# Decoder layer on one core: products with 64-row heads as two row tiles of TensorE, state sums as two column tiles, without zero-padded copies

## The chip, the cores and the metric

The kernel runs on one core of a Trainium2 chip. The metric is the time of one execution on the device in microseconds (us), lower is better; of several runs the median counts.

## The reference

One decoder layer over x of shape (8, 512, 256) in fp32: a gated slot attention with 4 heads of 64 and 64 slots, a cross attention with 16 heads of 16 over 64 keys for each batch, and a feed-forward part with 8 experts of which each token takes 2. Only the first two parts are touched. Cut to what matters:

```python
def step(carry, inp):                       # one token of the slot attention, for each of 4 heads
    hk, hv = carry
    q_t, k_t, v_t, s_t, g_t = inp
    ge = exp(g_t)
    hk = hk * ge[:, :, None, :] + k_t[..., :, None] * s_t[..., None, :]
    logits = einsum('bhk,bhkm->bhm', q_t * scale, hk)
    p = softmax(logits)
    hv = hv * ge[..., :, None] + s_t[..., :, None] * v_t[..., None, :]
    o_t = einsum('bhm,bhmv->bhv', p, hv)
...
scores = einsum('bhqd,bhkd->bhqk', Q, K) * scale + bias      # cross attention, 16 heads of 16
```

The kernel does the recurrence in chunks of 128 tokens. Inside a chunk the part `q k^T` of a head (causal, 128 tokens by 128) stands for the sum over earlier tokens, and likewise `p s^T` for the read of the values; what came before the chunk is held in the states hk and hv, two heads side by side as diagonal blocks of 64 by 64.

## The kernel before

The 4096 tokens are 32 chunks of 128 (`NCH`), four to a batch. The first stage loops over the chunks; the second, after it, runs the experts over 40 groups of 256 rows and isn't touched. Every engine has its own program, an order written out by hand: its `step(run)` lists the pieces of work of one chunk, and `run(lag, work)` does the piece for the chunk that lies `lag` behind. So one step of the loop does the slot attention of chunk n (lag 0 and 1), the cross attention of chunk n-1 and n-2, and the routing of n-3 and n-4. Steps are unrolled for the first 8 chunks; then a loop runs 6 times over 4 steps, and 4 last steps follow. Semaphores order the engines among each other; an engine never starts a piece before the one above it in its list.

In one step the slot attention of a chunk is a chain through all engines. VectorE (DVE) normalises the chunk (`f_xn`), TensorE (PE) turns and projects it, ScalarE (ACT) and DVE make the gates (`g_s`, `down`, `s_s`), PE turns k and s (`ks_columns`), ACT copies them out (`k_z`, `s_z`), PE makes the products `scores`, DVE masks them (`a_s`, line 902), PE makes `logits`, DVE and ACT the softmax (`lg`, `b_e`, `b_p`), PE turns `b_p` (`p_columns`), ACT copies it (`p_t`), PE makes the products `mix`, DVE masks them (`bt_s`, line 936), and PE makes `sum_states` and `read_out`. After `bt_s` DVE begins the next step with the statistics of the next chunk.

Heads have 64 rows, and a product over them is made with all 128 rows of the array: `k_z` and `s_z` hold one head each in a tile of 128 rows of which the other 64 are zeros, written once. The cross attention does the same with `k_bd`, in which GpSimd (POOL) lays the keys of 8 heads of 16 rows side by side, with zeros elsewhere; it is made once for each batch (`keys`, line 490). `sum_states` makes blocks of 128 by 128 of which only the diagonal blocks of 64 are used.

PSUM has eight banks, and `turns` says which results use a bank in which order; `bank_left` makes PE wait until the one before it has been read.

Of the kernel before, what the change touches and what calls it, by code (L numbers as in the profile page):

```python
# [29 lines left out]
ALU = mybir.AluOpType  # L30
ACT = mybir.ActivationFunctionType
AX = mybir.AxisListType
F32 = mybir.dt.float32
# [5 lines left out]
P = 128  # L39
# [33 lines left out]
def decoder_layer(nc, x, qpos, kpos, mask, ctx_t, wq, wk, wv, wf, gnorm, wo,  # L73
# [3 lines left out]
    with ctx:  # L77
# [18 lines left out]
        def part1(name, shape, dt=F32):  # L96
            return tiles1.enter_context(nc.sbuf_tensor(name, shape, dt))
# [7 lines left out]
        diag16 = part1("diag16", [P, HPT])  # L105
        pair_of = part1("pair_of", [P, 2])
# [34 lines left out]
        k_z, s_z = part1("k_z", [P, H, P]), part1("s_z", [P, H, P])  # L141
# [18 lines left out]
        k_bd = part1("k_bd", [P, KT, HPT, KL])  # L160
# [37 lines left out]
        bank = [ctx.enter_context(nc.psum_tensor(f"bank{i}", [P, 512], F32)) for i in range(8)]  # L198
# [11 lines left out]
        tile = {t: bank[i][:, :] for i, turn in enumerate(turns) for t, _ in turn}  # L210

# [7 lines left out]
        def sems(names):  # L219
            return [sem(t) for t in names.split()]  # L220
# [22 lines left out]
        down_ok, decay_ok, kz_ok = sems("down_ok decay_ok kz_ok")  # L243

        left = dict(f_cols=f_cols_ok, qk=qk_ok, vf=g_ok, gates=gates_ok, decay_cols=h_ok, ks_cols=ks_ok, sums=z_ok,
                    scores=a_ok, logits=lg_ok, p_cols=p_ok, mix=mix_ok, read=bo_ok, o_cols=o_ok, y=x1_ok,
# [68 lines left out]
        CONSTS = 15 + XH  # L315
# [105 lines left out]
        def _(pool):  # L421
# [34 lines left out]

            pool.wait_ge(consts_step, CONSTS)

# [118 lines left out]
        def _(act):  # L577
# [9 lines left out]
            def two(t):  # L587
                return t.rearrange("p (k t) -> p k t", k=2)
# [19 lines left out]
            def ks_columns(n, c, b):  # L608

                if later(n, 1):  # L610
                    act.wait_ge(mix_mm, n)
                else:
                    act.wait_ge(halves_zeroed, 6)
# [157 lines left out]
        def _(dve):  # L771
            for t in (k_z, s_z, *hk, *hv):
                dve.memset(t[:, :, :], 0.0).then_inc(halves_zeroed, 1)
# [55 lines left out]
            causal_h = causal[:, :].rearrange("p (a t) -> p a t", a=1).to_broadcast([P, H, P])  # L829
# [68 lines left out]
            def causal_scores(n, c, b):  # L898
                if later(n, 1):
                    dve.wait_ge(logits_mm, n)  # L900
                dve.wait_ge(scores_mm, n + 1)
                dve.tensor_tensor(a_s[:, :, :], tile["scores"].rearrange("p (h t) -> p h t", h=H), causal_h, ALU.mult)\
                   .then_inc(a_ok, 1)
# [91 lines left out]
            def x_scores(n, c, b):  # L995
                dve.wait_ge(bias_ok, n + 1)
                dve.wait_ge(xs_mm, n + 1)
                if later(n, 1):
                    dve.wait_ge(ex_ok, n)
                for k in range(2):  # L1000
                    last = dve.tensor_tensor(sc[:, 8 * k:8 * k + 8, :],
                                             tile[f"x_scores{k}"].rearrange("p (h k) -> p h k", h=HPT),
                                             bias[:, 8 * k:8 * k + 8, :], ALU.add)
                last.then_inc(sc_ok, 1)
# [220 lines left out]
        def _(pe):  # L1225
# [72 lines left out]
            def sum_states(n, c, b):  # L1298

                pe.wait_ge(v_ok, n + 1)  # L1300
                bank_left(pe, "sums", n)
                for m in range(2):
                    cols = slice(m * P, (m + 1) * P)
                    product(tile["sums"][:, cols], [(k_s[:, c % 2, cols], s_s[:, c % 2, cols])])
                    last = product(tile["sums"][:, D + m * P:D + (m + 1) * P], [(s_s[:, c % 2, cols], v_s[:, c % 2, cols])])
                last.then_inc(sums_mm, 1)

            def scores(n, c, b):
                pe.wait_ge(kz_ok, n + 1)
                bank_left(pe, "scores", n)  # L1310
                for h in range(H):
                    last = product(tile["scores"][:, h * P:(h + 1) * P], [(k_z[:, h, :], q_t[:, c % 2, h // 2, :])])
                last.then_inc(scores_mm, 1)
# [25 lines left out]
            def mix(n, c, b):  # L1339
                pe.wait_ge(p_ok, n + 1)  # L1340
                bank_left(pe, "mix", n)
                for h in range(H):
                    last = product(tile["mix"][:, h * P:(h + 1) * P], [(s_z[:, h, :], p_t[:, h // 2, :])])
                last.then_inc(mix_mm, 1)
# [31 lines left out]
            def x_scores(n, c, b):  # L1376

                pe.wait_ge(xq_ok, n + 1)
                pe.wait_ge(kbd_ok, b * KT + KT)
                for k in range(KT):  # L1380
# [154 lines left out]
```

## Time and profile before

| | |
|---|---|
| median of 3 runs | 1630.9 us (1628.46 to 1631.94) |
| span of the profiled execution, first to last instruction | 1613.6 us |
| busy in the span: PE, DVE, ACT, POOL | 88%, 65%, 41%, 28% |
| mean granted TensorE clock | 0.942 |

The span is 17.3 us below the median; that part lies before the first and behind the last instruction. The profiled execution has no total time of its own in the records besides its span. A chunk's step takes some 25 to 27 us, so the first stage is about 890 us of the span and the experts the rest. An fp32 product shows as two matmul records on PE (and two weight loads on PEld), so counts of PE rows are double the number of products. PE rows of the timeline give the start of a group of records, the time from its first start to its last end, and how many there are; the next row can start before that end, since matmuls overlap.

### The profile page before, as it was taken

What the parts mean: (1) busy time and instruction counts of PE and PEld (TensorE: products, weight loads), DVE (VectorE), ACT (ScalarE), POOL (GpSimd) and SP (SyncE); (2) the same over time, 40 slices, a digit from 0 to 9 for tenths busy, and PEclk for the clock granted to TensorE, in tenths of its full rate; (3) what the DMA queues carried; (4) which work ended last, traced back from release to release, by engine and by line L of the source; (5) the groups of instructions that cost most, each with busy time, mean ns of one, the idle gap of its engine ahead of it and who ended that gap; (6) DMA issues with size and microseconds to landing.
All of it is one profiled execution on the core that took longest, in us unless ns stands there. A gap on an engine that the chain in (4) does not pass through costs nothing. (4 is left out here: it accounts for less than half of the span.)

```text
span 1613.6 us, 31497 instructions
## 1 busy us (share of the span) xinstructions
PE 1425.9 (88%) x10360; PEld 1281.7 (79%) x10360; DVE 1049.4 (65%) x3246; ACT 656.3 (41%) x1626; POOL 446.7 (28%) x510
## 2 busy tenths in 40 slices
PE   6798988888888888888886499999999999999995
PEld 4576767767676667676775499999999999999995
DVE  3568787777788787878886465555555465555442
ACT  1345344444444343534342344444344344444331
POOL 1224233333333342423332211222121121222212
PEclk8899999998999999989997699999999999999998
DMA  9100000000000000000000513223141323241211
GB/s 311 53 9 29 15 29 15 29 15 28 15 28 19 24 27 15 28 14 29 14 21 12 195 27 86 58 54 93 29 116 29 107 38 108 38 109 28 40 21 20
DMA packets 65998, 79.65 MB, mean 49 GB/s; under 512 B 9793, under 2 KB 59330, under 8 KB 65856
## 3 DMA queue, kind: packets, MB, share of 16 engines
q1 hardware_dynamic: 51264, 59.05, 11.8%
q0 software_dynamic: 14592, 18.91, 7.0%
q8 instruction: 64, 1.05, 0.3%
q14 instruction: 78, 0.64, 0.1%
HBM read 44.15 MB, written 33.83 MB: 48 GB/s over the span
## 5 line engine op out<-in xcount | busy, mean ns | idle before, releaser
L755 ACT ACTIVATE h_a<-bank 128x256 f32<-128x256 f32 x320 | 122.5, 383 | 357.6 <-PE bank L1235 355.5
L1167 DVE TENSOR_TENSOR h_f<-bank,h_a 128x256 f32<-128x256 f32 x320 | 135.5, 424 | 156.5 <-ACT h_a L755 152.0
L461 POOL TENSOR_TENSOR idle_g<-half 128x1 f32<-128x1 f32 x112 | 23.5, 209 | 608.5 <-DVE y_s L1186 411.9
L1235 PE MATMUL bank<-xe_t_hi,w_even_hi 128*128 128x256 f32 x640 | 180.4, 282 | 0.0
L1235 PE MATMUL bank<-xe_t_hi,w_odd_hi 128*128 128x256 f32 x640 | 178.6, 279 | 0.0
L1235 PE MATMUL bank<-xe_t_lo,w_even_hi 128*128 128x256 f32 x640 | 178.5, 279 | 0.0
L1235 PE MATMUL bank<-xe_t_hi,w_even_lo 128*128 128x256 f32 x640 | 178.5, 279 | 0.0
L1235 PE MATMUL bank<-xe_t_lo,w_odd_hi 128*128 128x256 f32 x640 | 177.0, 276 | 0.0
L1235 PE MATMUL bank<-xe_t_hi,w_odd_lo 128*128 128x256 f32 x640 | 176.9, 276 | 0.0
L742 ACT ACTIVATE h_t_hi<-h_f 128x256 fp32r<-128x256 f32 x320 | 131.8, 412 | 28.8 <-DVE h_f L1167 28.7
L1174 DVE TENSOR_TENSOR h_t_lo<-h_f,h_t_hi 128x256 fp32r<-128x256 f32 x320 | 133.5, 417 | 6.1 <-ACT h_t_hi L742 5.0
L565 POOL DMA_INDIRECT out_dram<-y_s,token x80 | 125.2, 1565 | 27.3 <-issue 20.2
L1235 PEld LDWEIGHTS bank<-xe_t_lo,w_even_hi 128*128 128x128 f32 x640 | 122.0, 191 | 0.0
L1235 PEld LDWEIGHTS bank<-xe_t_hi,w_even_hi 128*128 128x128 f32 x640 | 121.9, 190 | 0.0
L1235 PEld LDWEIGHTS bank<-xe_t_hi,w_even_lo 128*128 128x128 f32 x640 | 121.8, 190 | 0.0
L1235 PEld LDWEIGHTS bank<-xe_t_hi,w_odd_hi 128*128 128x128 f32 x640 | 120.3, 188 | 0.0
L1235 PEld LDWEIGHTS bank<-xe_t_lo,w_odd_hi 128*128 128x128 f32 x640 | 120.3, 188 | 0.0
L1235 PEld LDWEIGHTS bank<-xe_t_hi,w_odd_lo 128*128 128x128 f32 x640 | 120.2, 188 | 0.0
L1235 PE MATMUL bank<-w_in,f_xnt 128*128 128x512 f32 (+1 forms) x256 | 99.7, 513 | 1.9 <-ACT f_xnt L585 1.9
L468 POOL TENSOR_TENSOR f_rstd<-f_var,neg_half 128x1 f32<-128x1 f32 x32 | 17.6, 551 | 291.2 <-DVE f_var L814 291.2
L1184 DVE CAST token<-about 128x1 uint32<-128x1 f32 x80 | 8.6, 149 | 130.8 <-PE bank L1235 130.8
L1235 PE MATMUL bank<-w_odd_hi,h_t_lo 128*128 128x256 f32 x320 | 88.5, 277 | 0.0
(220 smaller groups left out, 3961.8 us busy)
## 6 DMA issues: line engine op xcount, KB each, us to landing
raw<-in_w SPq DMA_DIRECT2D x24, 1024.0 KB, 8.5
expert_rows<-empty SPq DMA_DIRECT2D x4, 2580.0 KB, 21.5
xe<-expert_rows SPq DMA_DIRECT2D x40, 258.0 KB, 2.7
xin<-in_x SPq DMA_DIRECT2D x32, 128.0 KB, 2.3
out_dram<-x SPq DMA_DIRECT2D x32, 128.0 KB, 1.9
out_dram<-y_s,token POOLq DMA_INDIRECT x80, 3.8
mask_i<-in_mask SPq DMA_DIRECT2D x32, 32.0 KB, 1.7
expert_rows<-r_xn,send POOLq DMA_INDIRECT x64, 2.8
```

The costliest lines, as they stand in the source:

```text
L461: return pool.tensor_tensor(idle_g[:, i:i + 1], half[:, 0:1], half[:, 0:1], ALU.add)
L468: pool.tensor_tensor(rstd[:, :], var[:, :], neg_half[:, 0:var.shape[1]], ALU.pow).then_inc(done, 1)
L565: pool.indirect_dma_start(out=out, out_offset=bass.IndirectOffsetOnAxis(ap=token[par][a][:, :], axis=0), in_=y_s[:, par, a, :], in_offset= ...
L742: act.activation(h_t[0][:, par, f, :], h_f[:, f % 2, :], ACT.Copy).then_inc(h_hi_ok, 1)
L755: act.activation(h_a[:, f % 2, :], bank[2 + f % 4][:, 0:GS], ACT.Silu).then_inc(silu_ok, 1)
L1167: dve.tensor_tensor(h_f[:, f % 2, :], bank[2 + f % 4][:, GS:2 * GS], h_a[:, f % 2, :], ALU.mult)\
L1174: dve.tensor_tensor(h_t[1][:, par, f, :], h_f[:, f % 2, :], h_t[0][:, par, f, :], ALU.subtract)\
L1184: dve.tensor_copy(token[par][a][:, :], about[:, par, a, 0:1])
L1235: last = pe.matmul(dst, lhs, rhs, start=(i == 0), stop=(i == len(pairs) - 1))
```

## The change

The zero-padded copies go. `k_t` and `s_t` hold two heads on top of each other, rows 0 to 63 and 64 to 127, in one copy each. A product takes rows 0 to 63 or 64 to 127 of both operands, so that it uses one half of the array's rows (a row tile); two products next to each other in the program use different halves and write to different banks (`scores0`/`scores1`, `mix0`/`mix1`, `x_scores0`/`x_scores1`). `k_bd` has half as many columns, as 4 heads share a row half. The sums take 64 columns of weights and write 64 partitions, heads 0 and 2 to the lower, 1 and 3 to the upper half (a column tile). The blocks off the diagonal aren't written any more; the bank is zeroed once at the start. The turns of the banks change with the new names. DVE reads two banks in one operation (`two_banks`).

```diff
+        diag4 = part1("diag4", [P, HPT // 2])
-        k_z, s_z = part1("k_z", [P, H, P]), part1("s_z", [P, H, P])
+        k_t, s_t = part1("k_t", [P, PAIRS1, P]), part1("s_t", [P, PAIRS1, P])
-        k_bd = part1("k_bd", [P, KT, HPT, KL])
+        k_bd = part1("k_bd", [P, KT, HPT // 2, KL])
...
-            [("xo_cols", 3), ("qk", 0), ("scores", 0)],
+            [("xo_cols", 3), ("qk", 0), ("scores0", 0), ("mix0", 0)],
+            [("f_cols", 0), ("decay_cols", 0), ("scores1", 0), ("mix1", 0)],
             [("vf", 0), ("ks_cols", 0), ("logits", 0), ("r_cols", 3)],
             [("o_cols", 1), ("values", 2), ("sums", 0)],
-            [("f_cols", 0), ("decay_cols", 0), ("mix", 0)],
-            [("x_scores1", 2), ("p_cols", 0)],
-            [("x_scores0", 2), ("gates", 0), ("y", 1), ("e_cols1", 2), ("xq", 1)],
+            [("x_scores0", 2), ("p_cols", 0)],
+            [("x_scores1", 2), ("gates", 0), ("y", 1), ("e_cols1", 2), ("xq", 1)],
...
-                            .to_broadcast([P, HPT, KL]),
-                            diag16[:, :].rearrange("p (h a) -> p h a", a=1).to_broadcast([P, HPT, KL]),
+                            .to_broadcast([P, HPT // 2, KL]),
+                            diag4[:, :].rearrange("p (h a) -> p h a", a=1).to_broadcast([P, HPT // 2, KL]),
...
-                for t, dst, done in ((0, k_z, kz_ok), (1, s_z, ks_ok)):
-                    for i in range(2):
-                        rows = slice(M * i, M * i + M)
-                        last = act.activation(dst[rows, i::2, :], two(tile["ks_cols"][rows, t * D:(t + 1) * D]), ACT.Copy)
-                    last.then_inc(done, 1)
+                act.activation(k_t[:, :, :], two(tile["ks_cols"][:, 0:D]), ACT.Copy).then_inc(kt_ok, 1)
+                act.activation(s_t[:, :, :], two(tile["ks_cols"][:, D:2 * D]), ACT.Copy).then_inc(ks_ok, 1)
...
-                dve.tensor_tensor(bt_s[:, :, :], tile["mix"].rearrange("p (h t) -> p h t", h=H), causal_h, ALU.mult)\
+                dve.tensor_tensor(bt_s[:, :, :].rearrange("p (m i) t -> p i m t", i=2), two_banks, causal_h, ALU.mult)\
...
-                for m in range(2):
-                    cols = slice(m * P, (m + 1) * P)
-                    product(tile["sums"][:, cols], [(k_s[:, c % 2, cols], s_s[:, c % 2, cols])])
-                    last = product(tile["sums"][:, D + m * P:D + (m + 1) * P], [(s_s[:, c % 2, cols], v_s[:, c % 2, cols])])
+                for a, (keys, rows) in enumerate(((k_s, s_s), (s_s, v_s))):
+                    for h in range(H):
+                        i, cols = h % 2, slice(h * M, (h + 1) * M)
+                        last = product(tile["sums"][M * i:M * i + M, a * D + h * M:a * D + (h + 1) * M],
+                                       [(keys[:, c % 2, cols], rows[:, c % 2, cols])])
...
+            def by_pair(names, keys, queries):
+                for m in range(PAIRS1):
+                    for i in range(2):
+                        rows = slice(M * i, M * i + M)
+                        last = product(tile[names[i]][:, m * P:(m + 1) * P], [(keys[rows, m, :], queries[rows, m, :])])
+                return last
...
                 for k in range(KT):
-                    bank_left(pe, f"x_scores{k}", n)
-                    last = product(tile[f"x_scores{k}"], [(xq_t[:, k, :], k_bd[:, k, :, :].rearrange("p h k -> p (h k)"))])
+                    for i in range(2):
+                        rows = slice(P // 2 * i, P // 2 * (i + 1))
+                        last = product(tile[f"x_scores{i}"][:, k * D:(k + 1) * D],
+                                       [(xq_t[rows, k, :], k_bd[rows, k, :, :].rearrange("p h k -> p (h k)"))])
```

On PE, in a step with all lags, from the query projection of the cross attention (`x_xnt,xw`) to the turning of the next chunk (`ident,f_xn`), the program before reads so (out<-in, columns written; semaphores that a row waits for in brackets):

```order
L1235 MATMUL bank<-x_xnt,xw 128x128 x3
L1235 MATMUL bank<-p_t,s_z 128x128 [waits h_ok,mix_ok,f_cols_ok,p_ok]
L1235 MATMUL bank<-p_t,s_z 128x128 x3
L1235 MATMUL bank<-s_s,k_s 128x128 [waits xo_ok,z_ok,o_ok,v_ok]
L1235 MATMUL bank<-v_s,s_s 128x128
L1235 MATMUL bank<-s_s,k_s 128x128
L1235 MATMUL bank<-v_s,s_s 128x128
L1319 MATMUL bank<-hv,p_t 128x128 [waits bo_ok,et_ok,p_ok]
...
L1235 MATMUL bank<-k_bd,xq_t 128x512 [waits x1_ok,gates_ok,et_ok,sc_ok,xq_ok,kbd_ok]
L1235 MATMUL bank<-k_bd,xq_t 128x512 [waits p_ok,sc_ok]
L1229 MATMUL bank<-ident,f_xn 128x128 [waits h_ok,mix_ok,f_cols_ok,f_normed]
```

and with the change:

```order
L1239 MATMUL banks<-x_xnt,xw 128x128 x3
L1239 MATMUL banks<-p_t,s_t 128x128 [waits f_cols_ok,mix_ok,h_ok,a_ok,qk_ok,xot_ok,p_ok]
L1239 MATMUL banks<-p_t,s_t 128x128 x3
L1239 MATMUL banks<-s_s,k_s 64x64 [waits xo_ok,z_ok,o_ok,v_ok]
L1239 MATMUL banks<-s_s,k_s 64x64 x3
L1239 MATMUL banks<-v_s,s_s 64x64 x4
L1331 MATMUL banks<-hv,p_t 128x128 [waits bo_ok,et_ok,p_ok]
...
L1239 MATMUL banks<-k_bd,xq_t 128x256 [waits gates_ok,sc_ok,x1_ok,p_ok,et_ok,xq_ok,kbd_ok]
L1239 MATMUL banks<-k_bd,xq_t 128x256 x3
L1233 MATMUL banks<-ident,f_xn 128x128 [waits a_ok,h_ok,mix_ok,f_cols_ok,f_normed]
```

No piece changes its place: four `mix` products stay four, four sums of 128 by 128 become eight of 64 by 64, and two score products of 512 columns become four of 256.

On ACT, the copies of the turned k and s stood before between `ex` (the exponent of the cross attention) and `e_t`:

```order
L696 ACTIVATE ex<-sc 128x1024 [waits et_mm,scd_ok]
L618 ACTIVATE k_z<-bank 64x2x128 [waits ks_mm,mix_mm]
L618 ACTIVATE k_z<-bank 64x2x128
L618 ACTIVATE s_z<-bank 64x2x128 x2
L626 ACTIVATE e_t<-bank 128x512 [waits et_mm,av_mm]
```

and now:

```order
L696 ACTIVATE ex<-sc 128x1024 [waits et_mm,scd_ok]
L618 ACTIVATE k_t<-banks 128x256 [waits ks_mm,mix_mm]
L619 ACTIVATE s_t<-banks 128x256
L626 ACTIVATE e_t<-banks 128x512 [waits et_mm,av_mm]
```

Four copies over 64 rows have become two over 128 rows, in the same place.

## Rows read from the trace of the kernel before

**Rows 1.** Windows, both stages: window, us; busy (count) by engine; PEclk; DMA share, GB/s
```profile
60.00:860.00 800.00, 682.80 (x4188) 558.31 (x4188) 632.40 (x2134) 345.67 (x850) 278.81 (x289) 0.94 0.07 21
1000.00:1600.00 600.00, 594.83 (x5216) 594.43 (x5214) 318.68 (x810) 245.95 (x630) 127.30 (x144) 1.00 0.28 63
```

**Rows 2.** Line 936 (`bt_s`) on DVE over the whole span, and its idle time
```profile
L936 DVE TENSOR_TENSOR bt_s<-bank,causal x32: 690/692/692, 44.7 to 852.0; 128x512 f32<-128x512 f32 x32
...
  PE bank L1235: 62.9, 32
```

**Rows 3.** Timeline of DVE: start, duration, work, idle before and its releaser
```profile
404.42 0.69 DVE L936 TENSOR_TENSOR bt_s<-bank,causal 128x512 f32<-128x512 f32 x1 [2.87 <-PE bank L1235]
...
425.97 0.43 DVE L923 TENSOR_TENSOR b_p<-b_e,up 128x256 f32<-128x256 f32 x1 [0.55 <-ACT b_e L683]
428.79 0.69 DVE L936 TENSOR_TENSOR bt_s<-bank,causal 128x512 f32<-128x512 f32 x1 [1.04 <-PE bank L1235]
```

**Rows 4.** Timeline of PE from the query projection to the next chunk
```profile
401.28 1.91 PE L1235 MATMUL bank<-x_xnt,xw 128*128 128x128 f32 x8
402.99 1.32 PE L1235 MATMUL bank<-p_t,s_z 128*128 128x128 f32 x8
404.15 0.39 PE L1235 MATMUL bank<-s_s,k_s 128*128 128x128 f32 x2
...
406.33 1.94 PE L1235 MATMUL bank<-k_bd,xq_t 128*128 128x512 f32 x4
408.10 0.38 PE L1229 MATMUL bank<-ident,f_xn 128*128 128x128 f32 x2
```

**Rows 5.** Timeline of PE, the same place one step later
```profile
426.73 1.06 PE L1235 MATMUL bank<-x_xnt,xw 128*128 128x128 f32 x8
427.62 1.06 PE L1235 MATMUL bank<-p_t,s_z 128*128 128x128 f32 x8
```

**Rows 6.** Windows at these two places, columns as in rows 1
```profile
401.00:402.00 1.00, 1.00 (x7) 1.00 (x6) 0.51 (x2) 0.77 (x2) 0.00 (x0) 0.50 0.00 0
...
427.00:428.00 1.00, 1.00 (x12) 1.00 (x11) 0.68 (x3) 0.49 (x2) 0.00 (x0) 1.00 0.00 0
```

**Rows 7.** Line 902 (`a_s`) on DVE over the whole span, and its idle time
```profile
L902 DVE TENSOR_TENSOR a_s<-bank,causal x32: 690/691/692, 35.9 to 843.8; 128x512 f32<-128x512 f32 x32
...
  PE bank L1235: 2.9, 3
```

**Rows 8.** Groups by line and shape, 400 to 503 us: busy, mean ns, idle before
```profile
L1235 PE MATMUL bank<-s_s,k_s 128*128 128x128 f32 x16 | 3.1, 275 | 0.0
...
L1235 PEld LDWEIGHTS bank<-s_s,k_s 128*128 128x128 f32 x16 | 2.4, 192 | 0.0
```

**Rows 9.** Timeline of PE where it waits or slows inside a step
```profile
414.12 0.18 PE L1235 MATMUL bank<-both,before 128*128 128x8 bf16 x1 [1.20 <-DVE both L1082]
...
414.55 0.70 PE L1235 MATMUL bank<-g_s,tri_half 128*128 128x256 f32 x2 [0.23 <-DVE g_s L849]
...
418.99 1.16 PE L1235 MATMUL bank<-q_t,k_z 128*128 128x128 f32 x8 [0.36 <-ACT k_z L618]
...
423.70 0.44 PE L1229 MATMUL bank<-ident,x_xn 128*128 128x128 f32 x2 [0.99 <-DVE x_xn L818]
...
441.44 1.22 PE L1235 MATMUL bank<-g_s,tri_half 128*128 128x256 f32 x2 [0.23 <-DVE g_s L849]
```

**Rows 10.** Lines 490 (`k_bd`) and 513 (`bias`) on POOL, 983 (`hid`) on DVE
```profile
L490 POOL TENSOR_TENSOR k_bd<-k_all,diag x16: 1045/1066/1082, 53.4 to 788.7; 128x512 f32<-128x512 f32 x16
...
L513 POOL TENSOR_TENSOR bias<-dist,slopes x32: 1900/1902/2028, 64.0 to 867.5; 128x1024 f32<-128x1024 f32 x32
...
L983 DVE TENSOR_SCALAR hid<-mask_i x32: 182/184/1105, 62.1 to 865.9; 128x64 f32<-128x64 int32 x32
```

**Rows 11.** Timeline of POOL and DVE where both meet
```profile
470.30 2.08 POOL L490 TENSOR_TENSOR k_bd<-k_all,diag 128x512 f32<-128x512 f32 x2
...
471.35 1.09 DVE L983 TENSOR_SCALAR hid<-mask_i 128x64 f32<-128x64 int32 x1
```

More of the change, by code:

```diff
@@ L196, in decoder_layer @@
         y_s = sb("y_s", [P, 2, 2, D])
[L198 removed]
+        banks = ctx.enter_context(nc.psum_tensor("banks", [P, 8 * 512], F32))
+        bank = [banks[:, i * 512:(i + 1) * 512] for i in range(8)]
         turns = [
             [("counts", 4), ("e_cols0", 2), ("read", 0)],
[L202 removed]
+            [("xo_cols", 3), ("qk", 0), ("scores0", 0), ("mix0", 0)],
+            [("f_cols", 0), ("decay_cols", 0), ("scores1", 0), ("mix1", 0)],
             [("vf", 0), ("ks_cols", 0), ("logits", 0), ("r_cols", 3)],
             [("o_cols", 1), ("values", 2), ("sums", 0)],
[L205 to L207 removed]
+            [("x_scores0", 2), ("p_cols", 0)],
+            [("x_scores1", 2), ("gates", 0), ("y", 1), ("e_cols1", 2), ("xq", 1)],
             [("r_logits", 4), ("xy", 3), ("x_cols", 1)],
@@ L242, in decoder_layer @@
             "topi_ok both_ok gap_ok re_ok cnt_mm place_ok taken_ok slots_ok route_step halves_zeroed")
-        down_ok, decay_ok, kz_ok = sems("down_ok decay_ok kz_ok")
+        down_ok, decay_ok, kt_ok = sems("down_ok decay_ok kt_ok")
         left = dict(f_cols=f_cols_ok, qk=qk_ok, vf=g_ok, gates=gates_ok, decay_cols=h_ok, ks_cols=ks_ok, sums=z_ok,
-                    scores=a_ok, logits=lg_ok, p_cols=p_ok, mix=mix_ok, read=bo_ok, o_cols=o_ok, y=x1_ok,
+                    scores0=a_ok, scores1=a_ok, logits=lg_ok, p_cols=p_ok, mix0=mix_ok, mix1=mix_ok, read=bo_ok, o_cols=o_ok, y=x1_ok,
                     x_cols=x_cols_ok, xq=xq_ok, x_scores0=sc_ok, x_scores1=sc_ok, e_cols0=et_ok, e_cols1=et_ok,
@@ L771, in _ @@
         def _(dve):
-            for t in (k_z, s_z, *hk, *hv):
+            dve.memset(tile["sums"], 0.0)
+            for t in (*hk, *hv):
                 dve.memset(t[:, :, :], 0.0).then_inc(halves_zeroed, 1)
@@ L901, in causal_scores @@
                 dve.wait_ge(scores_mm, n + 1)
-                dve.tensor_tensor(a_s[:, :, :], tile["scores"].rearrange("p (h t) -> p h t", h=H), causal_h, ALU.mult)\
+                dve.tensor_tensor(a_s[:, :, :].rearrange("p (m i) t -> p i m t", i=2), two_banks, causal_h, ALU.mult)\
                    .then_inc(a_ok, 1)
@@ L999, in x_scores, with quarter @@
                     dve.wait_ge(ex_ok, n)
[L1000 to L1003, printed above, removed]
+                for i in range(2):
+                    def quarter(t):
+                        return t[:, :, :].rearrange("p (k i j) l -> p i k (j l)", k=KT, i=2)[:, i, :, :]
+                    last = dve.tensor_tensor(quarter(sc), tile[f"x_scores{i}"].rearrange("p (k n) -> p k n", k=KT),
+                                             quarter(bias), ALU.add)
                 last.then_inc(sc_ok, 1)
@@ L1301, in sum_states @@
                 bank_left(pe, "sums", n)
-                for m in range(2):
-                    cols = slice(m * P, (m + 1) * P)
-                    product(tile["sums"][:, cols], [(k_s[:, c % 2, cols], s_s[:, c % 2, cols])])
-                    last = product(tile["sums"][:, D + m * P:D + (m + 1) * P], [(s_s[:, c % 2, cols], v_s[:, c % 2, cols])])
-                last.then_inc(sums_mm, 1)
-            def scores(n, c, b):
[L1309 to L1313, printed above, removed]
+                for a, (keys, rows) in enumerate(((k_s, s_s), (s_s, v_s))):
[3 more added lines that the diff above has]
+                                       [(keys[:, c % 2, cols], rows[:, c % 2, cols])])
+                last.then_inc(sums_mm, 1)
+            def by_pair(names, keys, queries):
[4 more added lines that the diff above has]
+                return last
+            def scores(n, c, b):
+                pe.wait_ge(kt_ok, n + 1)
+                for name in ("scores0", "scores1"):
+                    bank_left(pe, name, n)
+                by_pair(("scores0", "scores1"), k_t, q_t[:, c % 2, :, :]).then_inc(scores_mm, 1)
             def with_states(dst, queries, states, weights, rows, weights_ok, n):
@@ L1340, in mix @@
                 pe.wait_ge(p_ok, n + 1)
[L1341 to L1344, printed above, removed]
+                for name in ("mix0", "mix1"):
+                    bank_left(pe, name, n)
+                by_pair(("mix0", "mix1"), s_t, p_t).then_inc(mix_mm, 1)
             def read_out(n, c, b):
@@ L1379, in x_scores @@
                 pe.wait_ge(kbd_ok, b * KT + KT)
+                for i in range(2):
+                    bank_left(pe, f"x_scores{i}", n)
                 for k in range(KT):
-                    bank_left(pe, f"x_scores{k}", n)
-                    last = product(tile[f"x_scores{k}"], [(xq_t[:, k, :], k_bd[:, k, :, :].rearrange("p h k -> p (h k)"))])
+                    for i in range(2):
+                        rows = slice(P // 2 * i, P // 2 * (i + 1))
+                        last = product(tile[f"x_scores{i}"][:, k * D:(k + 1) * D],
+                                       [(xq_t[rows, k, :], k_bd[rows, k, :, :].rearrange("p h k -> p (h k)"))])
                 last.then_inc(xs_mm, 1)
```

9 lines of the change are left out of this document (5 added, 4 removed).

## Prediction

> **What bounds the kernel now.** I read the windows first. From 60 to 860 us, the chunk stage, PE is busy 682.8 of 800 us (85%) and DVE 632.4 (79%); in the expert stage PE is busy 594.8 of 600 [rows 1]. The expert stage is PE's and isn't touched, so everything below is about the chunk stage. No engine is full there, so I looked for the loop that closes from step to step. It is in the order of DVE's work: `bt_s` is DVE's last piece of a step, the next chunk's statistics come behind it, and the chain of that next chunk leads back to its own `bt_s`. From `bt_s` at 404.42 to the start of `b_p` at 425.97 are 21.55 us, in which DVE works nearly without a pause; then 2.82 us pass until the next `bt_s` at 428.79, and here DVE waits for PE, 1.04 us in this step and 2.87 in the one before [rows 3]. Over all 32 chunks this wait is 62.9 us [rows 2]. So a step is a DVE part of about 22 us and a tail in which DVE waits: turn `b_p`, copy it, make the query projection that stands ahead of `mix` on PE, make `mix`.
>
> Why is that tail short once and long once? In the step at 427 us the eight records of the query projection take 0.89 us to the start of `mix`, 0.111 us each [rows 5]; at 401 us they take 1.71 us, 0.214 each [rows 4]. The granted clock is 1.00 in the one and 0.50 in the other, that is 2.4 and 1.2 GHz [rows 6]. Ahead of this place PE has sat idle 0.99 us for `x_xn`, earlier 1.20 us for `both` [rows 9]. If all 32 tails were like the short one, the waits would come to 32 x 1.04 = 33.3 us instead of 62.9; 29.6 us are the price of the low clock in the tail.
>
> What isn't on this loop: the `scores` products. DVE waited for them three times in 32, 2.9 us in all [rows 7].
>
> **The change part by part.** The sum is made against the span of 1613.6 us; the median of the runs, 1630.9, lies 17.3 us above it, and I keep those 17.3.
>
> *Keys on POOL.* `k_bd` takes 1.066 us for 512 columns, `bias` 1.902 for 1024 [rows 10]: 0.836 us for 512 more columns, so 256 columns should take 1.066 - 0.418 = 0.65 us, and the two `k_bd` of a batch 1.30 instead of 2.08. While they run, from 470.30 to 472.38, DVE's `hid` begins at 471.35 and takes 1.09 us [rows 11] where 0.184 is the median and 1.105 the most [rows 10]; it ends when `k_bd` does. `hid` is in the DVE part of the loop. With `k_bd` done 0.78 us earlier it ends 0.78 earlier. Once for each of the seven batches after the first: **-5.5 us**. Bounds: 0, if something else stops `hid`, and 7 x 0.91 = -6.4.
>
> *Copies on ACT.* Two copies of 128 rows for four of 64 rows free `scores` from its wait of 0.36 us [rows 9]. `scores` isn't on the loop [rows 7], so **0**. A new wait is in its list: `scores1` uses the bank of `decay_cols`, so PE now also waits for `start_states` on DVE. That work stands well ahead of `a_s` on DVE, so it can't delay `a_s`; what is queued behind `scores` on PE, the `e_columns` of the cross attention, would be late by tenths of a us and has slack. 0.
>
> *`mix` as row tiles.* This is the one product in the tail. It has eight records of 128 columns before and eight after, 0.89 us at the high clock [rows 5]. No row shows two products at once in different halves of the array. Bounds: if the second record of one product runs beside the first of the next, eight records take five places, 0.55 us, a gain of 0.34; if nothing overlaps, 0. Against it stands the change of the array's shape between `x_xnt,xw` and `mix`. A matmul record lasts 275 ns though the next starts 111 ns later, and its weight load 192 ns, normally hidden [rows 8]. If a change of shape makes PE let the last product run out, 275 - 111 = 0.16 us come into the open; if the load can't start before that either, 0.16 + 0.19 = 0.36 us. So a tail moves between -0.34 and +0.36 us. Taking half of each, -0.17 + 0.16, gives **0** for 32 steps, with -11 and +12 us as ends.
>
> The Trainium skill speaks on both sides here. "TensorEngine Tiling (Array Packing)", Key Properties, says that tiles run independently, and also that a change of the tiling mode, not merely of the tile, drains TensorE. It gives no price of the drain; no row here shows one. By the first sentence alone the step would gain the 0.34 us, by both together it comes near nothing.
>
> *The other products.* `x_scores`, four records of 512 columns, takes 1.77 us from 406.33 to 408.10 [rows 4]; with full overlap five places of half the length, 1.11 us. `sums`, eight records at 0.111 us, become sixteen short ones; between 0.45 us saved and nothing. `scores` like `mix`. A step enters or leaves a tiled shape seven times (into `x_scores` and out, into `scores` and out, into `mix`, on to `sums`, out): 7 x 0.16 = 1.1 to 7 x 0.36 = 2.5 us against 0.34 + 0.34 + 0.66 + 0.45 = 1.8 us saved at best. For PE's busy time that is about even. Its direct worth is 0: behind `mix` PE runs on to `both`, for which it waits 1.20 us anyway [rows 9]. That wait is also the cover if PE gets slower there.
>
> *DVE's operations* over two banks keep their count of elements and so, I take it, their 0.69 us [rows 2, 7]. The zeroing at the start is shorter by one operation, under cover of the loads. 0.
>
> Sum: 1613.6 - 5.5 = 1608.1 us span, and 1625.4 with the 17.3 around it.
>
> **The rivals.**
>
> *Overlap is full and the drain small.* The tail gains 0.34 x 32 = 11 us, with `k_bd` 16 us. At the low clock the saving in `mix` is double, and if the stretches of low clock fall on fewer tails, half of the 29.6 us can go as well: 1630.9 - 16 - 15 = 1600. For it: each product's halves are independent and write to different banks. Against it: the shapes change every few products.
>
> *PE gets faster, and the clock pays for it (the other side).* PE doesn't get more work, it waits longer. If `sums`, `x_scores` and `mix` are done 1.4 us earlier, the idle time ahead of `both` grows from 1.20 to 2.6 us, and with `scores` earlier that ahead of `x_xn` from 0.99 [rows 9] to 1.5 or more. In the step where PE had waited longer there, the gate product ran on for 1.22 us instead of 0.70 [rows 9]. A tail at the low clock costs 1.5 to 1.8 us more than one at the high clock [rows 3]. The waits tell that about 18 of 32 are low (29.6 / 1.65). If 10 more go low, +16.5; less 5.5, that gives 1642. It decides as soon as more than three tails are added (3.3 x 1.65 = 5.5). For it: a low clock follows idle PE in this trace, and this change makes PE idle where it doesn't bind. Against it: the drains may fill that idle time.
>
> *The changes of shape are dear.* With 0.36 us or more ahead of `mix` and little overlap the tail grows by 0.36 to 0.45 us: 32 x 0.4 = 13, less 5.5: 1638.
>
> *The tiles don't run beside each other and shape costs nothing.* Then PE does the same, and only `k_bd` counts, or even that is eaten by the stretches of low clock, which fall elsewhere when the step's length changes: 1625 to 1631.
>
> **How the numbers follow.** The forecast, the array part near nothing and `k_bd` 5.5 us, has a chance of 0.35, its own range 1615 to 1634, since the place of the low stretches shifts with any change of the step's length and three tails more or less are 5 us. Full overlap 0.17; the clock 0.30; dear changes 0.12; nothing but `k_bd` or not even that 0.06. The range of 1602 to 1650 leaves out the far end of the first rival and of the second. Faster by over 0.2% (3.3 us, about what a measurement of this kernel tells from no change): 0.24 + 0.17 + 0.02 + 0.03 = 0.46. Slower: 0.02 + 0.23 + 0.10 = 0.35. Within 0.2%: the remaining 0.19.
>
> **What the profile of the changed kernel would show.** `k_bd` near 0.65 us and `hid` near 0.2 to 0.3 in all steps: the first term. The start-to-start time of the `mix` records, 0.111 us at clock 1.00 now: about 0.06 means overlap; a gap of some tenths ahead of the first record of `mix`, `sums` and `hv,p_t` shows the changes of shape. DVE's wait ahead of `bt_s`, 62.9 us over 32: it gathers all of the tail; steps with a wait of 1.0 and of 2.5 or more tell the share of low clocks. `scores` without a wait for `k_t`, and no wait of DVE for `a_s`. I would be wrong in sign if the granted clock of the chunk stage falls clearly under 0.94 [rows 1], or if `bt_s` and `a_s` take longer than 0.69 us over two banks.

## The result and the profile after

The changed kernel takes 1649.89 us (median of 4, 1646.17 to 1655.04) against 1629.68 us of the kernel before (median of 4, 1626.49 to 1631.94). The ratio is 1.0096, with a 95% interval of 1.0059 to 1.0133 (the two medians divided give 1.0124, inside the interval): slower by 1%, where I had forecast faster by 0.34%. A run more than 1.5% above the fastest of the same kernel is left out of every ratio.

The profiled execution of the changed kernel has a span of 1644.4 us, 1.8 us under its own time of 1646.17, and a mean granted clock of 0.906 against 0.942. The chunk stage, columns as in [rows 1]:

```profile
60.00:860.00 800.00, 676.49 (x4438) 549.39 (x4436) 612.50 (x2069) 317.35 (x774) 265.06 (x281) 0.88 0.07 20
1000.00:1600.00 600.00, 595.18 (x5228) 594.99 (x5227) 323.40 (x816) 250.47 (x642) 124.94 (x141) 0.99 0.29 64
```

PE is busy for 676 of the 800 us (683 before), at a granted clock of 0.88 instead of 0.94. The wait of DVE ahead of `bt_s`, which gathers the tail [rows 2], grew:

```profile
L937 DVE TENSOR_TENSOR bt_s<-banks,causal x32: 690/692/693, 41.8 to 878.5; 128x512 f32<-128x512 f32 x32
...
  PE banks L1239: 76.1, 32
```

76.1 us instead of 62.9. Of the 32 waits that make it up, 29 are longer than 1.7 us, where 18 were; the others are 0.80 to 0.92 us, where they were 1.04 to 1.16. From the first `bt_s` to the last the changed kernel takes 29.4 us more (41.8 to 878.5, against 44.7 to 852.0), so this wait holds 13.2 us of it and not the whole. The next largest part is DVE's wait ahead of `s_s`, which stands behind PE's gate products (waits of DVE from 40 to 890 us: total, times, longest; before, then changed):

```profile
DVE s_s L868 <- issue: 7.4, 20, 0.5
...
DVE s_s L869 <- issue: 13.5, 16, 1.8
...
DVE s_s L869 <- ACT down L671: 2.9, 6, 1.6
```

That is 16.4 us instead of 7.4. Reading two banks at once costs nothing (0.692 us both). The keys and `hid`, over the whole span, answer to [rows 10]:

```profile
L495 POOL TENSOR_TENSOR k_bd<-k_all,diag x16: 612/640/650, 55.4 to 812.0; 128x256 f32<-128x256 f32 x16
...
L984 DVE TENSOR_SCALAR hid<-mask_i x32: 183/185/299, 65.3 to 892.0; 128x64 f32<-128x64 int32 x32
```

0.64 us for half the columns, and `hid` takes 0.30 us at most where it took 1.105: this term came as worked out. Now PE in one step of the changed kernel, which answers to [rows 4] and [rows 9] (64*128 and 128*64 are the rows and columns of the array that a product takes, where 128*128 is all of it):

```profile
400.70 0.18 PE L1239 MATMUL banks<-both,before 128*128 128x8 bf16 x1 [1.82 <-DVE both L1086]
...
405.44 0.71 PE L1239 MATMUL banks<-q_t,k_t 64*128 64x128 f32 x8 [0.23 <-DVE hv L887]
406.08 1.24 PE L1406 MATMUL banks<-ident,ex 128*128 128x128 f32 x8
...
408.16 0.66 PE L1336 MATMUL banks<-s_s,a_s 128*128 128x64 f32 x4 [0.61 <-DVE a_s L903]
...
410.48 0.54 PE L1233 MATMUL banks<-ident,x_xn 128*128 128x128 f32 x2 [0.99 <-DVE x_xn L819]
410.81 3.47 PE L1239 MATMUL banks<-v_bd,e_t 128*128 128x34 f32 x16
...
414.98 1.91 PE L1239 MATMUL banks<-x_xnt,xw 128*128 128x128 f32 x8
416.82 1.03 PE L1239 MATMUL banks<-p_t,s_t 64*128 64x128 f32 x8
417.78 0.45 PE L1239 MATMUL banks<-s_s,k_s 128*64 128x64 f32 x8
...
419.98 1.14 PE L1239 MATMUL banks<-k_bd,xq_t 64*128 64x256 f32 x8
421.04 0.44 PE L1233 MATMUL banks<-ident,f_xn 128*128 128x128 f32 x2
```

`x_scores` takes 1.06 us from 419.98 to 421.04, instead of 1.77, and `scores` 0.64 from 405.44 to 406.08, so tiles do run beside each other. PE then waits longer: 1.82 us for `both` instead of 1.20, 0.61 us for `a_s` and still 0.99 for `x_xn`. What follows is slow: the sixteen records of `v_bd` take 3.3 us to the next row and the projection 1.84. The windows there say why:

```profile
406.00:407.00 1.00, 1.00 (x11) 0.75 (x8) 0.96 (x4) 0.00 (x0) 0.56 (x1) 1.00 0.74 253
...
411.00:412.00 1.00, 1.00 (x8) 1.00 (x6) 0.93 (x3) 0.38 (x1) 0.00 (x0) 0.50 0.00 0
...
415.00:416.00 1.00, 1.00 (x6) 1.00 (x6) 0.24 (x1) 0.62 (x2) 0.00 (x0) 0.50 0.00 0
```

1.00 ahead of the waits, 0.50 (1.2 GHz) behind them. PE's work in the tail takes twice its time just where DVE waits for it.

Why does PE wait 0.99 us for `x_xn`, before and after? The prediction didn't ask. `x_xn` and `f_xn` are the same operation of DVE on the same shape, for two different inputs, and yet:

```profile
L819 DVE TENSOR_SCALAR f_xn<-xin,f_mv,f_rstd x32: 411/414/474, 22.3 to 853.4; 128x256 f32<-128x256 f32 x32
L819 DVE TENSOR_SCALAR x_xn<-x,x_mv,x_rstd x32: 406/2131/2141, 67.0 to 893.8; 128x256 f32<-128x256 f32 x32
...
408.30 2.13 DVE L819 TENSOR_SCALAR x_xn<-x,x_mv,x_rstd 128x256 f32<-128x256 f32 x1
...
408.38 1.90 POOL L518 TENSOR_TENSOR bias<-dist,slopes 128x1024 f32<-128x1024 f32 x1 [0.19 <-DVE dist L992]
```

`x_xn` takes 2.13 us where `f_xn` takes 0.41, while POOL makes `bias`; in 31 of the 32 chunks it lasts until 0.15 us behind the end of `bias`, which begins 0.1 us behind it at most; in the one chunk where `bias` begins 0.16 us behind it, it takes 0.41 us, and PE doesn't wait for it (28 and 4 of 32 in the kernel before). It is what the prediction had seen between `k_bd` and `hid` [rows 11], only larger and in nearly every step: POOL's `bias` makes the gap ahead of the tail. No run moves `bias`.

### The profile page after: what moved, and what is told of

Same layout as the page of the kernel before. It is cut to its first block and busy times, and to the rows that moved or that the text cites. A ratio compares the mean times of both kernels' runs of the same rounds, so it can differ in the third digit from the quotient of the medians.

```text
span 1644.4 us, 32252 instructions
## 1 busy us (share of the span) xinstructions
PE 1439.5 (88%) x10744; PEld 1289.9 (78%) x10744; DVE 1047.2 (64%) x3245; ACT 632.6 (38%) x1562; POOL 439.7 (27%) x511
## 3 DMA queue, kind: packets, MB, share of 16 engines
q8 instruction: 66, 1.08, 0.3%
## 5 line engine op out<-in xcount | busy, mean ns | idle before, releaser
L755 ACT ACTIVATE h_a<-banks 128x256 f32<-128x256 f32 x320 | 122.5, 383 | 360.8 <-PE banks L1239 360.8
L1171 DVE TENSOR_TENSOR h_f<-banks,h_a 128x256 f32<-128x256 f32 x320 | 135.6, 424 | 160.3 <-ACT h_a L755 155.9
L1239 PE MATMUL banks<-xe_t_hi,w_even_hi 128*128 128x256 f32 x640 | 180.6, 282 | 0.0
L1239 PE MATMUL banks<-xe_t_hi,w_odd_hi 128*128 128x256 f32 x640 | 178.6, 279 | 0.0
L1239 PE MATMUL banks<-xe_t_lo,w_even_hi 128*128 128x256 f32 x640 | 178.6, 279 | 0.0
L1239 PE MATMUL banks<-xe_t_hi,w_even_lo 128*128 128x256 f32 x640 | 178.5, 279 | 0.0
L1239 PE MATMUL banks<-xe_t_lo,w_odd_hi 128*128 128x256 f32 x640 | 177.0, 276 | 0.0
L1239 PE MATMUL banks<-xe_t_hi,w_odd_lo 128*128 128x256 f32 x640 | 176.9, 276 | 0.0
L1239 PEld LDWEIGHTS banks<-xe_t_lo,w_even_hi 128*128 128x128 f32 x640 | 122.2, 191 | 0.0
L1239 PEld LDWEIGHTS banks<-xe_t_hi,w_even_hi 128*128 128x128 f32 x640 | 122.2, 191 | 0.0
```

Source lines behind the costliest of these rows:

```text
L755: act.activation(h_a[:, f % 2, :], bank[2 + f % 4][:, 0:GS], ACT.Silu).then_inc(silu_ok, 1)
L1171: dve.tensor_tensor(h_f[:, f % 2, :], bank[2 + f % 4][:, GS:2 * GS], h_a[:, f % 2, :], ALU.mult)\
```

## The experiments

Theory 1: the tiles make PE quicker where it isn't the bound, it waits longer there, the clock falls behind the waits, and the tail pays. Theory 2: the shapes, the new waits for banks or the wider reads cost by themselves. The table holds, for the profiled execution of each kernel, the time at low clock (2 x (1 - granted clock), summed over windows of 1 us from 40 to 890 us), DVE's wait ahead of `bt_s`, and how many of its 32 parts are 1.7 us or longer. Each ratio is to runs of the kernel before made together with those of its line, and isn't the quotient of two medians; the medians of those runs went from 1629.05 to 1632.97 us, so medians of different lines compare to some 4 us only.

| kernel | median us | ratio to before, interval | low clock us | wait us | long waits |
|---|---|---|---|---|---|
| before (its shown profile) | 1629.68 | 1 | 128 | 62.9 | 18 |
| changed | 1649.89 | 1.0096 (1.0059 to 1.0133) | 222 | 76.1 | 29 |
| b_again, before once more (profile of its slowest run) | 1632.57 | 0.9997 (0.9956 to 1.0037) | 181 | 87.5 | 29 |
| a_fill, changed, fill 2 and 4 | 1613.84 | 0.9909 (0.9872 to 0.9945) | 51 | 28.3 | 1 |
| a_fill12, changed, fill 1 and 2 | 1575.38 | 0.9679 (0.9642 to 0.9716) | 91 | 33.7 | 5 |
| a_fill10, changed, fill 1 and 0 | 1606.67 | 0.9855 (0.9767 to 0.9942) | 157 | 41.4 | 11 |
| a_fill02, changed, fill 0 and 2 | 1633.34 | 1.0017 (0.9976 to 1.0058) | 201 | 75.5 | 30 |
| a_lower, as a_fill12, 64-row fill | 1578.86 | 0.9681 (0.9597 to 0.9765) | 104 | 38.9 | 9 |
| b_fill, before, fill 2 and 3 | 1613.50 | 0.9897 (0.9855 to 0.9940) | 34 | 37.9 | 2 |
| b_fill11, before, fill 1 and 1 | 1595.59 | 0.9804 (0.9766 to 0.9842) | 85 | 47.4 | 9 |
| b_mix, scores and mix tiled only | 1646.94 | 1.0108 (1.0064 to 1.0151) | 207 | 76.2 | 30 |
| b_xs, x_scores and keys only | 1634.28 | 1.0045 (1.0013 to 1.0077) | 188 | 83.3 | 26 |
| b_sums, sums only | 1628.16 | 0.9971 (0.9930 to 1.0013) | 159 | 72.9 | 23 |
| a_halves, other order of the tiles | 1654.75 | 1.0137 (1.0078 to 1.0195) | 222 | 74.7 | 30 |

**The kernel before once more (b_again).** No edit.

> The kernel before once more, unchanged, to see how far two executions of it differ. The profiled one of before had a span of 1613.6 us, 13 us under the lowest of its runs (1626.5). If spans and times differ by some 2 us, as in the changed kernel (1644.4 and 1646.2), that profiled execution was a quick one, and its neighbours should show spans of 1625 to 1630 at a clock under 0.942. Ratio to itself 1.00 within 0.004.

Nine of its ten runs went from 1616.48 to 1638.32 us, and the mean clock of a run moved with its time, though not in strict order: 1616.48 at 0.941, 1623.34 at 0.943, 1633.08 at 0.934, 1638.32 at 0.931. So the kernel before was already paying for the clock, by a varying amount, and the profile that I had read, span 1613.6, is of one of its quickest executions. Its time was about 1615, by the 1.8 us that lie around the span here, and not 1630.9.

The profile of this run is of the tenth, 1647.89 us at a clock of 0.922, and it is a warning: with no edit at all, 29 of its 32 waits ahead of `bt_s` are long and they add up to 87.5 us, more than in the changed kernel. One profile against another proves nothing here. What does tell is the clock of all runs: 0.905 to 0.911 in the four of the changed kernel, 0.931 to 0.943 in these nine of the kernel before.

**Fill on PE (a_fill, b_fill).** An fp32 product of 512 columns, run some times into a bank whose next result overwrites it, ahead of two waits; in the changed kernel 2 and 4, in the one before 2 and 3:

```diff
+            def fill(dst, times):
+                for _ in range(times):
+                    product(dst, [(ident[:, :], w_in[:, 0, 0:2 * D])])
...
-                pe.wait_ge(x_normed, n + 1)
                 bank_left(pe, "x_cols", n)
+                fill(tile["x_cols"], 2)
+                pe.wait_ge(x_normed, n + 1)
...
-                pe.wait_ge(both_ok, n + 1)
                 bank_left(pe, "counts", n)
+                fill(tile["counts"], 4)
+                pe.wait_ge(both_ok, n + 1)
```

> The changed kernel with extra fp32 products on PE where it sat idle: two of 512 columns (0.87 us) ahead of the wait for x_norm, four (1.74 us) ahead of the wait for both; they write into the bank that the next result overwrites. Nothing else differs. Theory 1, the low clock after idle PE is what costs: low-clock stretches go from 222 us to under 60, DVE's wait ahead of bt_s from 76.1 us to 32 x 0.8 = 26, the gates come at full clock, and the time falls below both kernels, to 1560 to 1600. Theory 2, the changes of shape or the new waits cost: the clock is no cause, the fill only adds to PE, and the time stays at 1646 or rises.

> The kernel before with two extra products ahead of the wait for x_norm and three ahead of that for both (it idles 1.20 us there). Theory 1: it has 128 us of low clock to lose, DVE's wait ahead of bt_s goes from 62.9 to 33 to 40, and the time falls to 1585 to 1610, above the changed kernel with its fill, since that one has the shorter mix (0.25 us in each of 32 steps) and keys. Theory 2: no change or slower.

Both fell to 1613, clearly under the kernel before, though PE had more to do; that is theory 1. Both missed the size, the changed kernel by 14 us, the one before by 3.5, and the reason stands in the rows of a_fill, of the tile `place` on DVE:

```profile
L1093 DVE TENSOR_TENSOR place<-banks,taken x32: 165/167/168, 129.1 to 897.2; 128x8 f32<-128x8 f32 x32
...
  PE banks L1239: 50.7, 32
```

and of `bt_s`:

```profile
  PE banks L1239: 28.3, 32
```

Only one of the 32 waits of the tail was still long, but I had priced a product at half of what it takes: it is two records of 0.43 us, 0.86 in all, so four are 3.44 us in a gap of 1.8, and `place` waited 50.7 us for the counts behind them (31.2 in b_fill).

**Shorter fill (a_fill12, b_fill11).** 1 and 2 products in the changed kernel, 1 and 1 in the one before.

> The changed kernel with a shorter fill: one product of 512 columns (0.86 us) ahead of the wait for x_norm, two (1.72 us) ahead of that for both. In the run before with two and four, four took 3.44 us and DVE's place waited 50.7 us for counts behind them, while DVE's wait ahead of bt_s was only 28.3 us. Theory 1 (the low clock costs): the low clock stays rare (under 80 us to 890 us), place waits under 10 us, and the time is 1570 to 1585. Theory 2 (something else in the change costs as well): it stays above 1600.

> The kernel before with one extra product ahead of the wait for x_norm and one ahead of that for both. Theory 1: place waited 31.2 us behind three of them; with one that goes, the clock stays high, 1580 to 1595. The changed kernel with its fill should be 8 to 15 us under it (mix 0.25 us x 32, keys 0.45 x 7, sums and x_scores nothing). Theory 2: this one is faster than the changed kernel with its fill.

1575.38 and 1595.59, as theory 1 has it (the second 0.6 us over its range; the low clock of the first 91 us, where I had expected under 80). Theory 2 is out as the cause of the loss: with the clock held for the most part, the changed kernel is 20.2 us faster than the one before, not slower. Each has the smaller of the two fills that it was tried with; the kernel before with 1 and 2 wasn't run, so 20.2 us holds for these two fills. The chunk stage of a_fill12 by windows:

```profile
60.00:860.00 800.00, 732.02 (x4863) 540.79 (x4862) 651.01 (x2234) 332.24 (x808) 286.85 (x304) 0.97 0.07 22
```

Its PE in a step:

```profile
655.77 1.08 PE L1239 MATMUL banks<-w_in,ident 128*128 128x512 f32 x2
656.93 0.44 PE L1233 MATMUL banks<-ident,x_xn 128*128 128x128 f32 x2
...
659.96 1.06 PE L1239 MATMUL banks<-x_xnt,xw 128*128 128x128 f32 x8
660.95 0.71 PE L1239 MATMUL banks<-p_t,s_t 64*128 64x128 f32 x8
661.59 0.45 PE L1239 MATMUL banks<-s_s,k_s 128*64 128x64 f32 x8
661.88 0.40 PE L1239 MATMUL banks<-v_s,s_s 128*64 128x64 f32 x8
662.21 0.49 PE L1336 MATMUL banks<-hv,p_t 128*128 128x128 f32 x2
...
663.79 1.13 PE L1239 MATMUL banks<-k_bd,xq_t 64*128 64x256 f32 x8
664.85 0.44 PE L1233 MATMUL banks<-ident,f_xn 128*128 128x128 f32 x2
```

and of b_fill11:

```profile
647.61 1.06 PE L1235 MATMUL bank<-x_xnt,xw 128*128 128x128 f32 x8
648.50 1.06 PE L1235 MATMUL bank<-p_t,s_z 128*128 128x128 f32 x8
649.39 0.39 PE L1235 MATMUL bank<-s_s,k_s 128*128 128x128 f32 x2
...
650.28 0.39 PE L1324 MATMUL bank<-hv,p_t 128*128 128x128 f32 x2
```

The same projection ahead of `mix` takes 0.99 us to the next row when a tiled product follows and 0.89 when a plain one does, and the medians over all steps whose tail has the full clock (27 and 24) are the same. So 0.10 us of the change of the array's shape stand ahead of the group. That isn't all of it: four pairs at the pace of 0.111 us would take 0.45, and `mix` takes 0.64, so about 0.2 us more lie inside the group and behind its last pair. `mix` takes 0.64 instead of 0.89 all the same, and the sums 0.62 instead of 0.89. A step saves 0.25 us in `mix`, 0.35 in `scores` (0.64 against 0.99), 0.27 in the sums and 0.71 in `x_scores`, 1.58 together, each read from the start of a group to the start of the next, so with all of the change of shape but the 0.10 ahead of it; those lie three times a step in the rows ahead, and 1.58 - 0.30, about 1.3 us a step, is what PE gains at full clock. Of the 20.2 us between the two kernels the waits ahead of `bt_s` are 47.4 - 33.7 = 13.7 and the keys 0.8 x 7 = 5.6, together 19.3; smaller terms of both signs stand beside them (`place` waits 7.9 us instead of 1.7, for one), so that the sum comes so near is in part luck.

**One place at a time (a_fill10, a_fill02).**

> The changed kernel with the one extra product ahead of the wait for x_norm alone. If the idle time ahead of x_xn is what lowers the clock in the tail, most of the 70 us go here: 1590 to 1610. If the idle time ahead of both counts as much, the gain is about half: 1605 to 1625.

> The changed kernel with the two extra products ahead of the wait for both alone. The tail comes behind the wait for x_xn, so its low clocks stay: 1620 to 1645. If both places count the same, 1605 to 1625.

Both came into the first of their ranges. Against 1649.89 the fill ahead of `x_norm` alone is worth 43 us, the one ahead of `both` alone 17, and both 75. The chunk stage, a_fill10:

```profile
60.00:860.00 800.00, 694.80 (x4652) 537.65 (x4651) 636.03 (x2164) 328.27 (x797) 277.96 (x294) 0.93 0.07 21
```

and a_fill02:

```profile
60.00:860.00 800.00, 724.97 (x4606) 568.04 (x4604) 622.91 (x2111) 321.62 (x786) 270.85 (x287) 0.89 0.07 21
```

PE is idle for 75 us in the second and for 105 in the first, and yet the clock of the second is the lower one: it counts where the idle time lies. (That PE is busier in the second is in part the low clock itself, which makes its work longer.) Each place has its own victim. The fill ahead of `x_norm` brings the wait ahead of `bt_s` to 41.4 us and leaves the one ahead of `s_s` (21.5 us, 16.4 without any fill). The fill ahead of `both` brings the wait ahead of `s_s` to 6.0 us, as the gate products stand right behind it, and leaves the one ahead of `bt_s` at 75.5 us with 30 long ones. So the gap ahead of `both` by itself isn't what slows the tails.

**The parts alone (b_mix, b_xs, b_sums).** Each is the kernel before with one part of the change; b_mix has the new copies on ACT and the new turns of the banks.

```diff
-                for h in range(H):
-                    last = product(tile["mix"][:, h * P:(h + 1) * P], [(s_z[:, h, :], p_t[:, h // 2, :])])
-                last.then_inc(mix_mm, 1)
...
+                by_pair(("mix0", "mix1"), s_t, p_t).then_inc(mix_mm, 1)
```

> Only scores and mix as row tiles, with the copies k_t and s_t and the new turns of the banks; x_scores, its keys and the sums as before. PE's products are 0.35 + 0.25 us shorter a step. Theory 1: idle ahead of both grows by 0.25 us, not by 1.2, so the clock falls only part of the way (0.94 to about 0.92) and the time is 1625 to 1640. Theory 2 (new waits for banks or shapes cost): the whole loss is here, 1645 to 1652.

> Only x_scores as row tiles, with the narrower keys on POOL. PE is 0.71 us shorter a step ahead of the wait for both, keys give DVE 0.9 us back in seven steps. Theory 1: the idle time ahead of both goes from 1.2 to 1.9 us and the clock falls: 1630 to 1645. Theory 2: x_scores is off the loop, so only the keys count: 1622 to 1626.

> Only the state sums as column tiles. They stand behind mix, and take 0.3 us less of PE's time a step. Theory 1 (PE's idle time lowers the clock): idle ahead of both grows by 0.3 us, a smaller step of the same kind as the other parts: 1629 to 1640. Theory 2 (column tiles or changes of shape cost nothing and gain nothing): 1627 to 1632.

The scores and `mix` alone bring a loss as large as the whole, +1.08%; `x_scores` with the keys +0.45%; the sums none that could be told (-0.29%, interval to +0.13%, and 1628.16 us is under the range of theory 1). b_mix came out where theory 2 had put it, by its number. But its profile goes with theory 1: the clock is at 0.89 (0.913 to 0.917 over the span in all seven runs), `mix` itself is quicker (0.64 us at full clock), and no wait for a bank stands among PE's waits. Its windows, then those of b_xs and b_sums:

```profile
60.00:860.00 800.00, 695.74 (x4088) 557.42 (x4087) 620.24 (x2087) 315.15 (x776) 271.64 (x282) 0.89 0.07 20
```

```profile
60.00:860.00 800.00, 683.59 (x4235) 574.25 (x4233) 617.04 (x2106) 345.65 (x846) 270.58 (x287) 0.90 0.07 21
```

```profile
60.00:860.00 800.00, 689.05 (x4403) 560.08 (x4401) 626.70 (x2117) 346.37 (x852) 277.49 (x287) 0.92 0.07 21
```

PE's idle time of the whole stage doesn't show the cause: it is 104 us in b_mix, 116 in b_xs and 111 in b_sums against 117 in the kernel before, since work at the low clock fills up what was idle. I had looked only at the gap ahead of `both` for b_mix. The waits of PE from 60 to 860 us show another place (before, then b_mix):

```profile
PE bank L1324 <- DVE a_s L902: 10.8, 14, 1.0
...
PE banks L1331 <- DVE a_s L902: 19.0, 22, 1.5
```

Quicker `scores` on earlier copies let PE reach the wait for `a_s` earlier, and this wait lies right ahead of the one for `x_xn` (28.8 us, 26.8 before), the place that a_fill10 shows to weigh most; the gap ahead of `both` is no longer than before (35.7 us, 39.6 before). That this is how b_mix loses is argued from these waits, not shown: b_mix with a fill wasn't run, and the profile of b_again has as many long tails with a wait for `a_s` of only 10.9 us.

**Do tiles run beside each other, and does their order matter (a_halves, a_lower)?** In a_halves the two products of one half come first, then those of the other:

```diff
-                for m in range(PAIRS1):
-                    for i in range(2):
+                for i in range(2):
+                    for m in range(PAIRS1):
```

> The changed kernel with the row tiles in another order: both products of the lower half, then both of the upper half, in scores, mix and x_scores. If halves run beside each other only when they alternate, the eight records of mix at full clock take about 0.9 us instead of 0.64 and x_scores 1.7 instead of 1.06. Theory 1: PE is longer at work and waits less, so the clock is a bit higher, and the time goes down or stays (1635 to 1650). Theory 2 (a drain with each change of tile or shape): there are fewer changes of tile, so PE is faster and the time falls by the changes saved, 6 a step x 0.16 us x 32 = 30 us at most.

```profile
406.28 0.72 PE L1239 MATMUL banks<-q_t,k_t 64*128 64x128 f32 x8 [0.26 <-DVE hv L887]
...
419.73 1.14 PE L1239 MATMUL banks<-k_bd,xq_t 64*128 64x256 f32 x8
```

The groups last 0.72 and 1.14 us as in the changed kernel (0.71 and 1.14). The order makes no difference to them, and so none to the time beyond the interval. Had the halves run beside each other only when they alternate, it would have been about 1.0 and 1.7. That left open whether a product of 64 rows is quicker by itself. a_lower is a_fill12 with the fill ahead of `x_norm` made of two products that use only rows 0 to 63:

```diff
-                fill(tile["x_cols"], 1)
+                for _ in range(2):
+                    product(tile["x_cols"][:, 0:D], [(ident[0:M, :], w_in[0:M, 0, 0:D])])
```

> As the best one so far (one and two extra products), but the one ahead of x_norm replaced by two products of 256 columns that use only rows 0 to 63. This measures whether a 64-row product is quicker by itself, or only beside one of the other half. Quicker only beside another: the four records take 0.85 us, as long as the two of 512 columns did, 0.213 each, and the time is that of the best, 1572 to 1582. Quicker by itself: about 0.12 us each, 0.48 in all, as in x_scores, where eight records take 1.06 us in either order of the halves.

```profile
661.03 1.13 PE L1239 MATMUL banks<-w_in,ident 64*128 64x256 f32 x4
...
662.09 0.44 PE L1233 MATMUL banks<-ident,x_xn 128*128 128x128 f32 x2
```

Four records of one half take 1.06 us to the next row, as long as eight of both halves in `x_scores`; less 0.1 at either end for the changes of shape 0.86, that is 0.21 each, the pace of a full-height record of 256 columns. A half alone is no quicker; two halves run side by side, in either order of issue. The time, 1578.86, is that of a_fill12 within its interval.

## Why the prediction was wrong

*What bounds the kernel.* Right: the loop from `bt_s` to `bt_s`, DVE's part and PE's tail, and the low clock as the reason for long and short tails. The fills show the price: a_fill12 has 131 us less of low clock than the changed kernel and takes 74.5 us less. Missing was where the gap of 0.99 us ahead of the tail comes from, POOL's `bias`.

*Keys on POOL.* Right in mechanism and size: 0.64 us where I had forecast 0.65, `hid` 0.30 at most.

*Copies on ACT, the new wait, DVE over two banks.* The durations were right. `scores1` does wait for `start_states` (0.23 us), and nothing on the loop feels it. But "isn't on the loop, so 0" is the first half of the step that failed: b_mix, where only these copies, `scores` and `mix` are changed, loses 1.08% although its `mix` is quicker, so what is off the loop isn't worth 0. That it works through PE's waits is argued above, not shown.

*`mix` as row tiles.* The mean of two bounds gave 0, and this term was mis-sized. The projection and `mix` together take 0.99 + 0.64 = 1.63 us instead of 1.78, and DVE's wait in a tail at full clock fell from 1.04 to 0.80, -0.24 us, as part of the change of shape comes behind the last pair. The overlap was fuller than my bound: the records of the two halves start 0.007 us apart in the trace, so eight records take four places and not five. The change of shape costs 0.10 us ahead of the group, under my lower bound of 0.16, and about 0.2 more inside and behind it, where I had looked for none. The Trainium skill's sentence that a change of mode drains TensorE ("TensorEngine Tiling (Array Packing)", Key Properties) goes with these 0.3 us, but it is no reason against this change.

*The other products: "its direct worth is 0".* This is the other half of the step, and with it the forecast went wrong in sign. I set PE's saved time about even with the shape changes (1.8 against 1.1 to 2.5 us) and called the wait ahead of `both` a cover. The saving is 1.3 us a step at full clock, the wait ahead of `both` is 1.82 us instead of 1.20, and the low clock behind PE's waits costs more than all the rest gives. I had this as the second rival, with its mechanism, its price (1642) and the point from which it decides (three more low tails). Its count was near: about 18 low tails and 10 more were forecast, 18 and 29 long waits are there. At its 1.65 us each the 11 more are 18 us, less 32 x 0.24 = 8 for the quicker `mix` 10, where the wait grew by 13. What it left out is the low clock in the DVE part of the loop, 9.0 us more ahead of `s_s`. Measured is 1649.89. Both profiles are single draws, as b_again shows, so these counts could have come out otherwise. The rival's chance of 0.30 was too low, because it hung on the same estimate of overlap and drain; with the overlap at its full and the drain small, the first rival's conditions, the second's outcome followed. The first rival had the clock improve instead, and its time of 1600 is off by 50 us for that reason. Which of the shortened pieces makes the additional long tails stays open; a_fill02, with the gap ahead of `both` filled and 30 long tails all the same, speaks against that gap.

*The base.* I took 17.3 us to lie around the span. It is 1.8; the other 15.5 were the difference between a quick execution and the median. The clock of one profile is one draw. With 0.942 I read the kernel before as paying 29.6 us in the tail; its median execution, at a clock of 0.93 to 0.94, pays more.

*What the profile would show.* I named a granted clock "clearly under 0.94" in the chunk stage as the sign of a wrong sign. It is 0.88.

## What to carry to other kernels

Before cutting work on TensorE ask whether it is the bound at that place. If not, the cut becomes a longer wait, and in a stage with gaps like those of 1.0 and 1.8 us here that can lower the clock of the work that is the bound. First hold the clock, for instance with spare products ahead of the waits that fit the gap (0.86 us each here, one and two of them), then cut: here that turned +1.0% into -3.2%, 1575.38 us, faster than both kernels; in the kernel before the fill alone gives -2.0% (1595.59). A fill that is longer than its gap costs again (1613.84). Ask also what makes the gap: here it is an operation of POOL that holds up one of DVE, and moving that might do without a fill. And read the granted clock of several executions, not of one profile.

## What was not expected of the hardware

- Two row tiles run side by side in fp32 even when both products of one half are issued first: eight records of 256 columns take 1.06 us alternating and 1.07 in the other order, four of one half alone 1.06.
- Going into a tiled shape and out again costs about 0.3 us here: 0.10 ahead (0.99 against 0.89 us for the same eight records ahead of `mix`) and about 0.2 inside and behind (`mix` takes 0.64 us, four pairs at the pace of 0.111 would take 0.45).
- Less idle time of PE can go with a lower clock: a_fill02 is idle 75 of 800 us at 0.89, a_fill10 105 us at 0.93.
- Executions of one unchanged kernel on one core differed by 1.4% (1616.48 to 1638.32 us), with the clock between 0.943 and 0.931.
- A DVE operation of 128x256 that takes 0.41 us takes 2.13 us beside POOL's `bias` of 1.90 us, and ends 0.15 us behind it.
